# More unread products in the waits, norm sums behind additions, and columns ahead of the last turn in a four-layer model kernel

## The chip, the cores and the metric

The kernel runs on one core of a Trainium2 chip, in one launch. The metric is the device time of that launch in microseconds (us). The engines are PE (TensorE, matrix products), DVE (VectorE), ACT (ScalarE), POOL (GpSimd) and SP (SyncE, which issues transfers). Each runs its own queue in order, and semaphores join them.

## The reference

The input is 4 batches of 512 tokens, each token a row of 64 numbers. Four layers follow an embedding of atoms and their neighbours. Each has an attention and a feed-forward part, both on the residual stream `h`:

```
h = h + attn(layernorm(h))
h = h + ffn(layernorm(h))
```

- Layer 0: a causal linear attention with 8 heads, then 16 experts of which each token takes two, and a norm of its own.
- Layer 1: a softmax attention with one head over 512 keys, whose batches the kernel takes in pairs ("two-head" below), then a gate from a graph attention over 262144 edges and 4 experts of which two count.
- Layer 2: an attention over keys and values of 4 channels each with a 4x4 product per head, then 8 experts, two per token.
- Layer 3: 8 heads of softmax attention, then a block with a causal attention of 4 heads and 8 gated experts, two per token.

## The kernel before, in words

Tokens lie on the 128 partitions in 16 tiles of 128 tokens; a batch ("quarter" `q`, 0 to 3) is 4 tiles. `H` is the residual stream, `X` the normed one, and `XT2` is X turned, with channels on the partitions. PSUM has 8 banks of 128x512 numbers. The order of the work is written out by hand on every engine.

**Unread products.** At many places PE makes products of the identity with itself, 128x128 by 128x512 in bf16, that nobody reads (`dense` in `entry`, `unread` in the attentions). They keep PE active in a wait. They stand in PE's queue like any other product, so what follows must let them finish.

**`entry`** (line 2301) is what comes before a layer part: the norm in steps on DVE and ACT, the turn of X (L2534) and for experts the router or gate product (L2542). PE issues `dense` products first, then some after each step of quarter 0 (L2547). For experts, DVE then finds the two best experts and makes three bf16 terms of their weights (L2463, L2466), and PE turns the weights (L2584). Before that turn stands `turn_gates`: PE waits until DVE's steps for half 0 have come to `count - k` for k in 20, 14 and 8, and makes two unread products after each.

**`experts`** (line 1433) runs 4 x T tiles of experts in pairs: hidden layer (L1474), gates spread over the rows (L1485), ACT's function (L1543), DVE's product with the gate (L1571) and the second product (L1505). At the end of a quarter DVE sums two halves (L1577), PE turns them (L1512) and DVE adds them to the residual (L1562, L1564). If a norm follows (`after`), DVE makes its sums for quarter q (L2241, L2243) and later its root (L2260, L2262), and POOL centres, squares, takes the power and multiplies (L2251, L2254, L2269, L2272). So the first three quarters of the next norm are made within the experts, and the last quarter after them, with the last turn (`last_turn`).

**`softmax_attention`** (line 189) is the attention of layer 1: 2 groups `g` of 2 batches, 4 chunks `c` of 128 keys or queries each, step `s = 4g + c`. `rows` (L303) makes products whose maxima DVE takes (L488). After 4 chunks DVE splits the maxima in three bf16 terms (L497 to L505), PE turns them (`maxima`, L317), and ACT copies them (L432). `cols` (L329, L335) makes the products again, turned, with the maximum subtracted; ACT takes exponentials (L455), and `mix` (L351) multiplies by the values. `proj` (L291) makes queries and keys of a group from XT2, and needs both batches turned; the batches of group 1 are `first` (2) and `later` (3, the one whose norm ends last). `outs` (L362) is the head's output product. PSUM banks are given in the order of a list `units`, three pairs of banks in turn.

**`linear_attention`** (line 1158) handles 8 groups: products of keys and queries per chunk (`diagonals`, L1229), a turn of the keys (L1236), the running state (L1243), outputs within a chunk and across (L1254, L1263), and the head product (L1276).

**`l2_attn`** (line 3273): `kv(q)` (L3299) makes keys and values of a quarter, DVE adds a bias (L3459), ACT squares (L3405), DVE sums and scales (L3463 to L3472). `schedule` is the list of these steps.

## Time and profile before

| | |
|---|---|
| median of 3 runs | 909.41 us (908.62 to 911.94) |
| the profiled execution | 908.61 us, span 906.8 us |
| PE busy | 794.8 us, 88% of the span, 9110 products |
| DVE busy | 641.0 us, 71% |
| ACT busy | 367.0 us, 40% |
| POOL busy | 241.0 us, 27% |
| mean granted TensorE clock | 0.957 of 2.4 GHz |

The span runs from the first to the last instruction; what lies around it is 1.8 us. Busy shares are means over stages with different limits. Where PE is busy nearly without gaps and the granted clock is below full, its products themselves are slower. An unread product counts as busy.

### The profile page before, as it was taken

How to read it: one execution, taken by the hardware profiler on the slowest of the kernel's cores; microseconds unless marked ns; L12 is line 12 of the kernel's file. 1: busy time of each engine (PE TensorE's matmuls, PEld its weight loads, DVE VectorE, ACT ScalarE, POOL GpSimd, SP SyncE). 2: the span in 40 equal slices, each digit the busy share in tenths (PEclk: the TensorE clock that was granted, in tenths of full speed). 3: DMA queues.
4: the chain of work that ended last, by engine and by line, in shares of the span. 5: the costliest groups of instructions: out<-in, count | busy, mean ns of one | idle time of the engine just before them, and what ended most of it. 6: DMA issues, size and time to landing. Idle time of an engine off the chain costs nothing. (4 is left out here: it accounts for less than half of the span.)

```text
span 906.8 us, 21880 instructions
## 1 busy us (share of the span) xinstructions
PE 794.8 (88%) x9110; PEld 417.8 (46%) x9110; DVE 641.0 (71%) x1720; ACT 367.0 (40%) x633; POOL 241.0 (27%) x308
## 2 busy tenths in 40 slices
PE   0897879979999887997978989999999988888997
PEld 0566757755544335774445423333333333344443
DVE  3988648887897448998776885556565557666665
ACT  0213354444664243323444614555554432353443
POOL 1900003222645212441362041113133325110000
PEclk9898989998999999999899999999999999987999
DMA  9500030000000001000000000000000000000000
GB/s 280 170 1 2 1 98 3 3 3 2 1 2 2 1 2 50 1 2 1 1 1 2 1 2 1 1 3 2 1 2 1 2 1 3 3 2 1 7 7 13
DMA packets 11501, 15.40 MB, mean 17 GB/s; under 512 B 8390, under 2 KB 9446, under 8 KB 10406
## 3 DMA queue, kind: packets, MB, share of 16 engines
q1 hardware_dynamic: 9984, 12.91, 4.6%
q8 instruction: 72, 1.18, 0.5%
q10 hardware_dynamic: 1418, 1.09, 0.5%
q14 instruction: 27, 0.22, 0.1%
HBM read 13.47 MB, written 0.52 MB: 15 GB/s over the span
## 5 line engine op out<-in xcount | busy, mean ns | idle before, releaser
L1001 DVE TENSOR_REDUCE mx<-PS 128x2 f32<-128x1024 f32 (+3 forms) x96 | 103.1, 1088 | 65.8 <-PE PS L776 54.6
L947 ACT ACTIVATE arena<-PS 128x1024 f32<-128x1024 f32 (+3 forms) x96 | 85.8, 917 | 119.4 <-PE PS L820 107.7
L810 PE MATMUL PS<-arena 32*64 32x512 f32 (+3 forms) x768 | 86.3, 563 | 8.8 <-DVE mx L1001 2.9
L836 PE MATMUL PS<-arena 128*64 128x512 f32 (+3 forms) x384 | 91.1, 558 | 0.4 <-DVE arena L1060 0.4
L776 PE MATMUL PS<-arena 32*64 32x512 f32 (+3 forms) x768 | 85.6, 563 | 0.9 <-DVE mx L1001 0.4
L1543 ACT ACTIVATE arena<-PS,f_b_sb 128x512 f32<-128x512 f32 x96 | 61.1, 684 | 39.6 <-PE PS L1474 36.9
L1571 DVE TENSOR_TENSOR arena<-arena,PS 128x512 f32<-128x512 f32 x96 | 61.6, 683 | 15.6 <-PE PS L1485 15.5
L1474 PE MATMUL PS<-XT,late 64*64 64x512 f32 x384 | 63.0, 619 | 2.9 <-issue 1.5
L1505 PE MATMUL PS<-arena,late 64*64 64x512 f32 x384 | 57.9, 595 | 0.0
L1105 POOL TENSOR_TENSOR H<-H,arena 128x256 f32<-128x256 f32 x32 | 23.5, 733 | 114.3 <-DVE arena L1035 111.8
L1755 DVE TENSOR_TENSOR arena<-arena,PS 106x512 f32<-106x512 f32 (+1 forms) x48 | 30.8, 684 | 20.9 <-PE PS L1655 13.7
L810 PEld LDWEIGHTS PS<-arena 32*64 32x64 f32 x768 | 19.1, 130 | 55.9 <-issue 32.1
L2073 PE MATMUL PS<-late 128*128 128x128 fp8e5 x512 | 35.6, 234 | 8.4 <-DVE late L1982 8.4
L1723 ACT ACTIVATE arena<-PS 106x512 f32<-106x512 f32 (+1 forms) x48 | 26.0, 594 | 39.9 <-PE PS L1643 39.9
L2547 PE MATMUL PS<-identh 128*128 128x512 bf16 x80 | 27.4, 493 | 14.8 <-PEq L1198 4.0
L836 PEld LDWEIGHTS PS<-arena 128*64 128x64 f32 x384 | 19.7, 135 | 44.7 <-issue 38.5
L2073 PEld LDWEIGHTS PS<-late 128*128 128x128 fp8e5 x512 | 32.7, 106 | 13.2 <-DVE late L1982 11.1
L2269 POOL TENSOR_TENSOR st<-st,Cc 128x4 f32<-128x4 f32 x24 | 24.4, 1018 | 41.3 <-DVE st L2262 41.3
L3048 POOL TENSOR_TENSOR arena<-NB,vals 128x1280 f32<-128x1280 bf16 x11 | 25.7, 2339 | 34.9 <-DVE vals L3123 34.9
L1396 POOL TENSOR_TENSOR H<-H,arena 128x256 f32<-128x256 f32 x28 | 20.4, 728 | 53.4 <-DVE arena L1359 51.2
L1060 DVE SCALAR_TENSOR_TENSOR arena<-arena,Cc 128x256 f32<-128x256 f32 x32 | 15.5, 495 | 23.2 <-ACT arena L947 23.0
L1643 PE MATMUL PS<-XT,late 64*64 64x512 f32 (+1 forms) x192 | 30.4, 605 | 1.0 <-DVE L L2369 1.0
(482 smaller groups left out, 1718.4 us busy)
## 6 DMA issues: line engine op xcount, KB each, us to landing
arena<-in_rel SPq DMA_DIRECT2D x4, 1024.0 KB, 11.9
late<-in_edges SPq DMA_DIRECT2D x2, 1024.0 KB, 11.8
arena<-in_adj SPq DMA_DIRECT2D x1, 1024.0 KB, 6.8
late<-in_w_f_w SPq DMA_DIRECT2D x2, 512.0 KB, 3.9
Cc<-in_consts SPq DMA_DIRECT2D x1, 916.0 KB
arena<-in_ids ACTq DMA_DIRECT2D x1, 800.0 KB
late<-in_w_f_w SPq DMA_DIRECT2D x2, 340.0 KB, 3.7
late<-in_w_f_w SPq DMA_DIRECT2D x4, 128.0 KB, 2.9
```

The lines of the kernel that those rows point to most:

```text
L776: ins = nc.tensor.matmul(PS[half(m), a + j, keys(g, c)], QT[h, g % 3, of_chunk(c, m)], KT[h, g % 3, keys(g, c)], start=True, stop=not late ...
L810: ins = nc.tensor.matmul(PS[half(m), a + j, queries(g, c)], KT[h, g % 3, of_chunk(c, m)], QT[h, g % 3, queries(g, c)], start=not less_firs ...
L836: ins = nc.tensor.matmul(PS[half(j), 6 + p, queries(g, c)], XO[:, batch(g) * TB + c, :], PT[:, s % 2, p, j, queries(g, c)], start=c == 0, ...
L947: nc.scalar.activation(PT[:, s % 2, p, :, queries(g, c)], PS[:, a:a + 2, queries(g, c)], ACT.Exp, scale=of(g).scale).then_inc(exp_done.sem, 1)
L1001: v.reduce_max(mx[:, g % 2, c, 2 * p:2 * p + 2], PS[:, a:a + 2, keys(g, c)], axis=AX.X).then_inc(max_done.sem, 1)
L1474: ins = nc.tensor.matmul(PS[half(m), up_bank(n), :], w1(i)[r, half(m)], XT2[r, b * S:(b + 1) * S], start=True, stop=True, skip_group_check ...
L1505: ins = nc.tensor.matmul(PS[half(i), banks[m], :], w2(i)[half(m)], HG[half(m), n % 4, :], start=m == 1 and i < 2, stop=i >= T - 2, skip_gr ...
L1543: nc.scalar.activation(HA[:, n % 3, :], PS[:, up_bank(n), :], act_fn, bias=b1(tiles[n][1])).then_inc(hidden_done.sem, 1)
L1571: v.tensor_tensor(HG[:, n % 4, :], HA[:, n % 3, :], PS[:, gate_bank(n), :], ALU.mult).then_inc(gated_done.sem, 1)
L1643: ins = nc.tensor.matmul(PS[m, z, :], w1(*tile)[half(z), m], XT2[half(z), b * S:(b + 1) * S], start=True, stop=True, skip_group_check=True)
L1755: nc.vector.tensor_tensor(HG[0:rows_of(r), n % 4, :], HA[0:rows_of(r), n % 3, :], PS[0:rows_of(r), 2 + z, :], ALU.mult).then_inc(gated_don ...
L2073: ins = nc.tensor.matmul(PS[:, 6 + m % 2, n * P:(n + 1) * P], spelt[k % 3][:, g, P:2 * P], spelt[k % 3][:, g, 0:P], start=g % GROUP == 0, ...
```

## The change

- `entry`: 8 unread products at the head instead of 4, unless there are two norms with a sum (5 there, as before). This touches five of the entries.
- `turn_gates`: unread pairs after seven marks, k = 20, 14, 12, 10, 8, 6, 4, instead of three; 14 products instead of 6, in all four expert layers.
- `linear_attention`: 14 unread products instead of 8 ahead of the first group, and 4 more between its diagonals and its turn.
- `experts` with 4 tiles per quarter (layers 1 and 2): the norm's sums stand right behind the addition of their quarter, and no longer behind the gating and the summing of that turn of the loop.
- `softmax_attention`: the order is written for two groups. The maxima are turned, and two steps of columns made, before `later` is turned and group 1 projected. 3 unread products stand in the first wait instead of 6. ACT takes the exponentials of steps 0 and 1 ahead of the copies for group 1. POOL copies values of batches 0 and 1 between its steps of the last norm.
- `l2_attn`: quarter 2 is turned behind `kv(1)` and the queries, ACT copies it behind the first square, and the root of the last norm stands one step earlier in DVE's queue.

```diff
@@ softmax_attention, the order of PSUM banks
+        first, later = new_in(1)
+        units = [("N", q, 0) for q in new_in(0)] + [("P", 0, 0)] + [("A", s, 0) for s in range(TB)]
+        units += [("N", first, 0), ("T", 0, 0), ("B", 0, 0), ("B", 1, 0), ("N", later, 0), ("P", 1, 0)]
+        units += [("B", 2, 0), ("A", TB, 0), ("A", TB + 1, 0), ("B", 3, 0), ("A", TB + 2, 0), ("A", TB + 3, 0), ("T", 1, 0)]
+        units += [("B", TB, 0), ("B", TB + 1, 0), ("O", 0, 0), ("B", TB + 2, 0), ("B", TB + 3, 0), ("O", 1, 0)]
@@ softmax_attention, PE
                 for s in range(TB):
                     rows(s)
-                first, later = new_in(1)
                 entered.turn(eng, first, slot(("N", first, 0)))
-                unread(6, a=7)
-                entered.turn(eng, later, slot(("N", later, 0)))
+                unread(3, a=7)
                 maxima(0)
-                proj(1)
                 eng.wait_ge(out_added.sem, before["out_added"])
                 eng.wait_ge(xo_ready.sem, at(xo_ready, 1))
...
+                cols(0)
+                cols(1)
+                mix(0, 0)
+                entered.turn(eng, later, slot(("N", later, 0)))
+                proj(1)
+                cols(2)
+                mix(1, 0)
+                rows(TB)
+                rows(TB + 1)
+                cols(3)
+                mix(2, 0)
+                rows(TB + 2)
+                rows(TB + 3)
+                mix(3, 0)
+                maxima(1)
+                for s in range(TB, U):
+                    cols(s)
+                    if s > TB:
                         mix(s - 1, 0)
...
+                    if s == TB + 1:
+                        outs(0, 0)
+                mix(U - 1, 0)
@@ softmax_attention, ACT
+                    if s == 1:
+                        entered.turned_out(eng, later, bank(("N", later, 0)))
+                        qk(1)
+                    if s == 3:
+                        contexts(0)
+                        maxima(1)
@@ softmax_attention, POOL
-                if len(entered.norms) > 1:
-                    entered.centre(eng, B - 1, 1)
-                    entered.apply(eng, B - 1, 1)
-                for b in range(B):
+                values_out(0)
+                entered.centre(eng, B - 1, 1)
+                values_out(1)
+                entered.apply(eng, B - 1, 1)
+                for b in range(2, B):
                     values_out(b)
@@ linear_attention, PE
-                unread(8, 6)
+                unread(14, 6)
...
                     diagonals(g)
+                    if g == 0:
+                        unread(4, 6)
                     turn(g)
@@ experts, DVE
+        short = T == 2 * LAG
...
                         v.tensor_tensor(dst[:, y, :], turned[:, :, 1], dst[:, y, :], ALU.add).then_inc(out_added.sem, 1)
+                        if after is not None and short and b < B - 1:
+                            eng.wait_ge(out_added.sem, a0 + b + 1)
+                            after.sums(eng, b, 0)
...
-                            if e == 0:
+                            if e == 0 and not short:
@@ entry, PE
-                    dense(5 if len(norms) > 1 and norms[0].plus is not None else 4)
+                    dense(5 if len(norms) > 1 and norms[0].plus is not None else 8)
...
-                    for k in (20, 14, 8):
+                    for k in (20, 14, 12, 10, 8, 6, 4):
                         eng.wait_ge(gate_steps[0].sem, gate_steps[0].count - k)
                         dense(2)
@@ l2_attn, PE
                 kv(0)
-                entered.turn(eng, 2, turn_bank(2))
                 kv(1)
                 queries(0)
                 queries(1)
+                entered.turn(eng, 2, turn_bank(2))
                 kv(2)
@@ l2_attn, ACT
-                for q in range(B - 1):
+                for q in range(2):
                     entered.turned_out(eng, q, turn_bank(q))
...
+                        if q == 0:
+                            entered.turned_out(eng, 2, turn_bank(2))
@@ l2_attn, DVE
-                    if (k, q) == (2, 0):
+                    if (k, q) == (1, 0):
                         entered.root(eng, B - 1, 0)
```

The order of PE's queue in the two-head attention, from the first turn for group 1 to the rows of its first two steps. Names are those of the code: `Cc,X` is a turn of X, `identh` alone an unread product, `XT,late` the projection. Before:

```order
L2294 MATMUL PS<-Cc,X 64x128 x8
L368 MATMUL PS<-identh 128x512 x6
L2294 MATMUL PS<-Cc,X 64x128 x8
L317 MATMUL PS<-identh,arena 128x128 x4
L291 MATMUL PS<-XT,late 64x512 x4
L329 MATMUL PS<-arena 64x512 x4
L335 MATMUL PS<-arena,minus 64x512 x4
L303 MATMUL PS<-arena 64x512 x8
```

In the changed kernel, whose own line numbers stand here (L2263, L348, L297, L271, L309, L315, L331 and L283 are the lines above, with L331 the `mix`):

```order
L2263 MATMUL PS<-Cc,X 64x128 x8
L348 MATMUL PS<-identh 128x512 x3
L297 MATMUL PS<-identh,arena 128x128 x4
L309 MATMUL PS<-arena 64x512 x4
L315 MATMUL PS<-arena,minus 64x512 x4
L309 MATMUL PS<-arena 64x512 x4
L315 MATMUL PS<-arena,minus 64x512 x4
L331 MATMUL PS<-arena 64x512 x4
L2263 MATMUL PS<-Cc,X 64x128 x8
L271 MATMUL PS<-XT,late 64x512 x4
```

The second turn and the projection moved from ahead of the first columns to behind two steps of them and one `mix`.

The order of ACT's queue in the key-value attention, from its first copy. `XT<-PS` is the copy of a turned quarter, `arena<-arena` the square. Before:

```order
L2299 COPY XT<-PS 128x512 x3
L3405 ACTIVATE arena<-arena 128x512
L3414 ACT_TABLE_LOAD
L3414 ACTIVATE chan<-chan 128x128
L3405 ACTIVATE arena<-arena 128x512
```

In the changed kernel:

```order
L2268 COPY XT<-PS 128x512 x2
L3374 ACTIVATE arena<-arena 128x512
L2268 COPY XT<-PS 128x512
L3385 ACT_TABLE_LOAD
L3385 ACTIVATE chan<-chan 128x128
L3374 ACTIVATE arena<-arena 128x512
```

The third quarter's copy moved behind the first square, still ahead of the table load.

PE's queue at the gates of the second expert layer, between the first hidden products and the first spread of gates. Before:

```order
L1474 MATMUL PS<-XT,late 64x512 x6
L2547 MATMUL PS<-identh 128x512 x6
L2584 MATMUL PS<-identh,G 64x128 x32
L1485 MATMUL PS<-GT,pickh 64x512 x4
L1474 MATMUL PS<-XT,late 64x512 x2
```

In the changed kernel:

```order
L1440 MATMUL PS<-XT,late 64x512 x6
L2516 MATMUL PS<-identh 128x512 x14
L2553 MATMUL PS<-identh,G 64x128 x32
L1451 MATMUL PS<-GT,pickh 64x512 x4
L1440 MATMUL PS<-XT,late 64x512 x2
```

Eight unread products more stand ahead of the turn of the gates; nothing else moved.

## Rows read from the trace of the kernel before

**Rows 1.** Stretches: window, length, busy (count) PE PEld DVE ACT POOL, PEclk, DMA share, GB/s

```profile
125.00:131.80 6.80, 5.58 (x23) 3.56 (x25) 4.60 (x10) 1.66 (x4) 0.00 (x0) 0.50 0.11 24
...
210.30:217.10 6.80, 6.80 (x49) 2.65 (x40) 5.80 (x40) 2.85 (x6) 0.00 (x0) 0.50 0.01 2
...
302.50:305.90 3.40, 3.22 (x18) 1.33 (x18) 0.00 (x0) 1.12 (x2) 0.95 (x5) 0.50 0.00 0
...
428.80:435.60 6.80, 6.13 (x58) 3.21 (x62) 4.69 (x14) 3.33 (x7) 1.21 (x5) 0.50 0.01 2
...
811.00:817.80 6.80, 6.00 (x39) 3.84 (x39) 5.88 (x20) 4.12 (x11) 0.00 (x0) 0.50 0.01 2
...
824.70:834.90 10.20, 7.82 (x58) 3.57 (x55) 6.78 (x39) 3.92 (x7) 0.00 (x0) 0.50 0.01 2
```

**Rows 2.** Timeline: start, length, engine, line, operation, count [idle before]; norm before linear attention

```profile
109.92 2.33 PE L2547 MATMUL PS<-identh 128*128 128x512 bf16 x10
...
111.89 0.40 DVE L2353 TENSOR_TENSOR X<-tA,st 128x256 f32<-128x256 f32 x1
...
112.34 3.71 PE L2534 MATMUL PS<-Cc,X 128*64 128x128 f32 x64
```

**Rows 3.** Timeline, linear attention, its first group, PE

```profile
119.52 1.90 PE L1268 MATMUL PS<-identh 128*128 128x512 bf16 x8
...
123.39 1.17 PE L1229 MATMUL PS<-arena 32*128 32x128 f32 x32 [1.97 <-DVE arena L1342]
...
125.66 0.90 PE L1236 MATMUL PS<-Cc,arena 128*128 128x128 f32 x3 [1.09 <-DVE arena L1342]
...
127.12 1.76 PE L1243 MATMUL PS<-arena 128*128 128x192 f32 x6 [0.57 <-ACT arena L1320]
```

**Rows 4.** Timeline, PE in the gates of the first expert layer

```profile
212.68 2.74 PE L2547 MATMUL PS<-identh 128*128 128x512 bf16 x6
...
215.35 1.91 PE L2584 MATMUL PS<-identh,G 128*64 128x128 bf16 x32
```

**Rows 5.** Timeline, two-head attention, PE and one row of DVE

```profile
296.76 1.47 PE L368 MATMUL PS<-identh 128*128 128x512 bf16 x6
...
301.71 1.30 PE L2294 MATMUL PS<-Cc,X 128*64 128x128 f32 x16 [3.48 <-POOL X L2272]
...
302.19 0.27 DVE L505 CAST arena<-mrest 128x8 bf16<-128x8 f32 x1
...
315.22 1.04 PE L329 MATMUL PS<-arena 64*64 64x512 f32 x8
...
317.91 0.38 PE L317 MATMUL PS<-identh,arena 128*128 128x128 bf16 x4 [0.58 <-DVE arena L505]
...
318.97 1.09 PE L329 MATMUL PS<-arena 64*64 64x512 f32 x8 [0.68 <-ACT arena L432]
```

**Rows 6.** Timeline, PE in the gates of the second expert layer

```profile
429.47 1.92 PE L2584 MATMUL PS<-identh,G 128*64 128x128 bf16 x32 [1.11 <-DVE G L2463]
...
435.59 0.59 PE L1505 MATMUL PS<-arena,late 64*64 64x512 f32 x2
```

**Rows 7.** Timeline, PE in the gates of the third expert layer

```profile
501.85 2.44 PE L2547 MATMUL PS<-identh 128*128 128x512 bf16 x6
...
504.22 1.08 PE L2584 MATMUL PS<-identh,G 128*64 128x128 bf16 x32
...
508.27 0.59 PE L1505 MATMUL PS<-arena,late 64*64 64x512 f32 x2
```

**Rows 8.** Timeline, ACT and PE in the key-value attention

```profile
460.83 0.58 ACT L2299 COPY XT<-PS 128x512 f32<-128x512 f32 x1 [3.37 <-PE PS L2294]
...
466.20 1.09 PE L2294 MATMUL PS<-Cc,X 128*64 128x128 f32 x16 [1.28 <-POOL X L2272]
```

**Rows 9.** Timeline, PE in the norm and the gates of the last expert layer

```profile
814.12 3.68 PE L2534 MATMUL PS<-Cc,R 128*64 128x128 f32 x32 [0.23 <-DVE R L2355]
...
828.55 1.92 PE L2584 MATMUL PS<-identh,G 128*64 128x128 bf16 x32 [0.95 <-DVE G L2463]
```

79 lines of the change are left out of this document (6 added, 73 removed).

## The prediction

> **What bounds the kernel now.** I read the page's busy shares first: PE is busy for 88% of the span, so the end is set by PE nearly everywhere, and what counts is where PE waits and how fast its clock is. The slices of the granted clock show short dips, and the view of stretches places them [rows 1]. In each of these six the granted clock is 0.50, which is 1.2 GHz, and PE is busy for 35.6 of their 40.8 us. I then read the timeline around each, to see what PE did just before the clock fell. Each time it had waited: for DVE in the linear attention [rows 3], 3.48 us for POOL's last norm in the two-head attention [rows 5], for DVE's gate steps in the experts [rows 6, 9]. So the change is worth what it takes from waits and from half-clock work, less what its own products hold up.
>
> **Prices.** Eight unread products take 1.90 us and six 1.47 at full clock [rows 3, 5], so one more costs (1.90 - 1.47) / 2 = 0.215 us. At half clock six take 2.74 [rows 4], some 0.43 us each without the tail.
>
> **1. Norm ahead of the linear attention, +4 products.** Ten unread products end at 112.25, X is ready at 112.29, and the turn starts at 112.34 [rows 2]. The last product's tail overlaps its follower by some 0.2 us, so about 0.26 us is spare. 4 x 0.215 = 0.86, less 0.26: **+0.6 us**. Ends: 0 if PE has more slack, +0.9. In the other four entries the products stand before a turn that ACT's copies, behind a table load, or DVE's steps hold up anyway: 0; were that cover gone, +0.6 each.
>
> **2. Linear attention, +6 and +4 products.** They stand in waits of 1.97 and 1.09 us [rows 3]; 6 x 0.215 = 1.29 and 4 x 0.215 = 0.86 fit, so nothing is held up. Behind them comes the half-clock stretch from 125.0, with PE busy 5.58 of 6.8 us [rows 1]. At full clock half of that goes, 2.8 us at most; L1243 alone would fall from 1.76 us to 0.9 [rows 3]. Part of it lies beside ACT and DVE. **-2.0**, ends 0 and -2.8.
>
> **3. Gates of the first expert layer, +8 products.** Here the clock is at half from 210.3 to 217.1 [rows 1], because of a wait ahead of L1474 that the change leaves alone. The six products start at 212.68 and the turn follows at once, at 215.35 [rows 4]: no room is left. Fourteen make ten by 217.1, and four at full clock end at about 217.9. The turn then takes 1.08 instead of 1.91 us [rows 4, 7] and ends at 219.0, not at 217.26: **+1.7**. All eight at half clock would cost 3.4; with full clock from the start they fit into DVE's steps, 0.
>
> **4. Two-head attention, new order.** PE now waits 3.48 us for the turn of `later`, and the split of the maxima ends at 302.46 [rows 5]. In the new order `maxima(0)` is next, and it cannot start before 302.5 whatever the order, since DVE's split stands behind POOL's norm as before. With 3 unread products instead of 6 PE runs dry at about 297.6 and waits 4.9 us. The maxima come 0.4 us earlier, but at 302.5 the turn, most of it done before, is still to be made (-0.4, +0.8). New waits: the first columns wait for ACT's copy of the maxima, 0.7, like the 0.68 in front of the later columns [rows 5], where the projection used to fill in; the projection waits for ACT's copy of the turn, 0.58 for a copy [rows 8], 0.5 taken. At `maxima(1)`, columns and `mix` of step 3 stood between the last rows and the turn, 2.1 us from 315.22, and 0.58 were left [rows 5]. Now only `mix(3)`, some 0.9, stands there, and two rows in a row make DVE's maxima later by 0.4: a wait of 2.0. Against this, `mix(4)` no longer waits (-0.4). Sum: -0.4 + 0.8 + 0.7 + 0.5 + 1.4 - 0.4 = 2.6, and I take **+2.5**. Ends: -0.4, if the queues behind PE take up all the waits, and +4.2, with another half-clock stretch behind the second wait (half of 3.22 us of PE work [rows 1]).
>
> **5. Gates of the second expert layer.** Of the eight new products two go before 425.3 and six after 427.3, in waits. The turn starts at 429.47 after an idle 1.11 us for DVE's G [rows 6], so they hold nothing up. From its start to L1505 it is 6.12 us at half clock [rows 6], and 4.05 in the third layer at full clock [rows 7]. **-2.0**, ends 0 and -2.1.
>
> **6. Layer 1 experts into key-value attention.** The sums behind the addition put the norms of quarters 1 to 3 about 1.3 us ahead, while L1571 and L1577 come 0.6 later, where PE has other work. ACT no longer waits 3.37 us for the turn of quarter 2 before its first square [rows 8]. The last turn, at 466.20 after 1.28 us for POOL [rows 8], comes some 2.7 earlier, but DVE's chain is the bound from there: **-1.4**, ends 0 and -3. What is late next is `kv(3)`. In layer 2 the same move gains about 1 us for the norms, but its one early turn and the last turn wait for the sum that now comes later: 0, ends -0.5 and +0.8.
>
> **7. Gates of the third expert layer.** As in 3: six products from 501.85, the turn at 504.22 without a wait [rows 7]. Eight more, four of them at half clock or so: **+1.6**, ends 0 and +3.4.
>
> **8. Norm of the last expert layer, +4.** They stand in a wait, and the turn that follows takes 3.68 us at a granted clock of 0.50 [rows 1, 9], about 1.9 at full. **-1.6**, ends 0 and -2.0.
>
> **9. Gates of the last expert layer.** The products run until about 829.1, past 828.55 (+0.55), where the turn now starts after 0.95 us idle [rows 9]. But PE is busy 7.82 of 10.2 us at half clock here [rows 1], and some 4.5 of that would be at full clock: **-1.7**, ends +1.6 and -3.0.
>
> Sum: 0.6 - 2.0 + 1.7 + 2.5 - 2.0 - 1.4 + 0 + 1.6 - 1.6 - 1.7 = -2.3 us. The profiled execution took 908.61 us, so 906.3; the median of the runs is 0.8 above it, so the forecast is **907.1 us**.
>
> **A rule on the clock.** In this trace the half clock comes behind waits, though not behind every one: the 3.48 us wait brought it, the waits around 317 did not [rows 1, 5]. The Trainium skill (TensorE: Matmul & The Clock Gate, Part 1: The HAM clock gate) says that the activity is measured in a free-running period that does not start with the kernel, so that the same kernel turns slow or fast at other points from run to run. One trace cannot show it. By it terms 3 and 7 could be 0 in one run and 3.4 in the next; this speaks against more products where the clock may be low, and is the first rival.
>
> **The rivals.** (a) *The slow stretches lie elsewhere.* If the clock is full at 212 and 501, the fourteen products fit into DVE's steps, terms 3 and 7 are 0, and PE gains another half microsecond in each. With -2.8 in term 2, +1.5 in term 4, -2.1 in 5 and -2.4 in 9 the sum is 0.6 - 2.8 - 0.5 + 1.5 - 2.1 - 1.4 - 0.5 - 1.6 - 2.4 = -9.2: 900.2 us. For it: three of these are already the mild end of their rows. Against it: the waits ahead of terms 3 and 7 are untouched. (b) *The two-head attention loses more: slower.* The longer wait of 4.9 us and the new one of 2.0 ahead of `maxima(1)` each end in a half-clock stretch, and term 4 is +4.2. It decides from the point where the second wait passes about 2 us, against 0.58 now [rows 5]; if then the products of 2, 5, 8 and 9 bring only a half of their gain, the sum is 0.6 - 1.0 + 1.7 + 4.2 - 1.0 - 1.4 + 1.6 - 0.8 - 0.4 = +3.5, and with term 3 and 7 at their ends (+3.4) +7.0: 916.4 us. (c) *The change does not lift the clock.* The stretches stay where they are, terms 2, 5, 8 are 0 and 9 is +1.0: 0.6 + 1.7 + 2.5 - 1.4 + 1.6 + 1.0 = +6.0, 915.4 us. Against it: in term 2 the unread products nearly fill the waits ahead of the stretch.
>
> **How the numbers follow.** The forecast has a chance of 0.54, (a) 0.28, (b) 0.10, (c) 0.08. A measurement of this kernel can tell about 0.5%, 4.5 us, from no change: faster is below 904.9, slower above 913.9. All of (a) and little of the forecast's own lower flank are faster, 0.30; (c) and (b) lie about that upper bound, and half of their milder forms fall below it: slower 0.11; the rest, 0.59, within. The range reaches from 901.5, near (a), to 912.5, short of (b) and (c).
>
> **What the changed profile would show.** Right: granted clock 1.0 in the first group of the linear attention, behind the gates of the second and last expert layers and in the last norm's turn; two-head columns that start at about 303.8 on this trace's scale, but a wait of some 2 us before the second turn of maxima; the kv attention's last turn without a wait for POOL. The unread products of the first and third gates end after DVE's G is ready. Wrong: a two-head attention that is no longer than before, which would mean that PE was not its bound; or a mean clock still at 0.957.

## The result, and the profile after

The changed kernel is slower: a median of 913.83 us over 20 executions against 909.46 for the kernel before, ratio 1.0047 (95% interval 1.0027 to 1.0067), so +4.3 us where -2.3 was forecast. The executions of the changed kernel lie between 907.4 and 918.5 us, those of the kernel before between 903.5 and 918.1 us. Ratios here and below compare fast executions only, that is, those within 1.5% of the fastest of the same kernel. The profiled one took 917.40 us, span 915.6. Its page, the busy shares and the slices of the granted clock:

```profile
span 915.6 us, 21998 instructions
...
PE 812.5 (89%) x9169; PEld 426.2 (47%) x9169; DVE 641.4 (70%) x1720; ACT 367.2 (40%) x633; POOL 243.3 (27%) x308
...
PEclk9886999989999798999998898999999999998999
```

PE is busy for 17.7 us more than before. To see where, I cut both traces at the same products: without the unread ones both kernels issue the same 8920, in another order only inside the two stages that were rewritten. A stretch is what lies between two such cuts. Here is the view of stretches before, its columns as in [rows 1]. The rows are, in this order, the norm ahead of the linear attention, the latter's first groups, norm and gates of layer 0, the two-head attention, the graph attention's first part, the gates of layer 1, its experts and the key-value attention, the gates of layer 2, its last experts, the attention of layer 3, and norm and gates of its experts:

```profile
99.49:112.83 13.34, 10.73 (x136) 8.08 (x137) 9.46 (x42) 5.99 (x18) 1.99 (x1) 1.00 0.01 1
112.83:137.68 24.85, 19.72 (x252) 14.05 (x252) 12.34 (x23) 13.30 (x25) 1.16 (x2) 0.86 0.30 89
...
190.30:232.38 42.08, 34.85 (x387) 20.84 (x381) 32.29 (x139) 20.59 (x39) 13.68 (x10) 0.88 0.01 2
...
282.88:331.02 48.14, 41.49 (x398) 17.29 (x394) 20.63 (x42) 16.50 (x23) 15.42 (x27) 0.96 0.00 1
331.02:373.15 42.13, 34.20 (x369) 24.59 (x369) 36.98 (x115) 14.76 (x34) 12.69 (x13) 0.96 0.09 28
...
408.00:443.82 35.82, 31.28 (x216) 16.09 (x217) 28.22 (x138) 14.83 (x26) 8.10 (x20) 0.90 0.00 1
443.82:495.62 51.80, 42.25 (x404) 24.86 (x398) 38.05 (x87) 22.93 (x47) 23.47 (x26) 0.93 0.01 1
495.62:525.81 30.19, 28.18 (x270) 13.66 (x270) 24.64 (x113) 15.58 (x26) 3.94 (x6) 0.94 0.00 1
525.81:543.99 18.18, 15.97 (x120) 4.91 (x116) 15.03 (x26) 3.32 (x6) 6.97 (x15) 1.00 0.01 1
543.99:805.33 261.34, 247.76 (x3360) 89.73 (x3364) 156.95 (x290) 117.44 (x153) 68.86 (x94) 0.99 0.01 2
805.33:843.87 38.54, 31.90 (x280) 17.45 (x273) 26.90 (x130) 15.18 (x31) 0.00 (x0) 0.78 0.01 1
```

The same stretches after:

```profile
104.01:118.04 14.03, 11.50 (x140) 8.47 (x141) 10.12 (x45) 6.67 (x19) 1.99 (x1) 1.00 0.00 1
118.04:140.36 22.32, 19.45 (x263) 13.38 (x262) 11.66 (x20) 12.69 (x24) 1.16 (x2) 1.00 0.32 100
...
192.94:235.42 42.48, 36.29 (x399) 21.39 (x393) 32.26 (x139) 20.60 (x39) 13.68 (x10) 0.88 0.01 2
...
285.89:338.82 52.93, 42.47 (x395) 18.27 (x391) 20.41 (x42) 16.65 (x23) 15.43 (x27) 0.90 0.00 1
338.82:382.05 43.23, 36.15 (x372) 25.83 (x373) 36.95 (x115) 14.76 (x34) 12.69 (x13) 0.92 0.08 27
...
416.88:450.71 33.83, 30.75 (x223) 15.62 (x224) 28.17 (x138) 14.62 (x26) 8.07 (x20) 1.00 0.01 1
450.71:501.28 50.57, 43.50 (x408) 25.26 (x402) 39.57 (x87) 23.16 (x47) 23.46 (x26) 0.90 0.00 1
501.28:535.18 33.90, 31.17 (x279) 14.54 (x278) 26.53 (x118) 15.58 (x26) 5.17 (x8) 0.90 0.01 1
535.18:552.65 17.47, 16.01 (x118) 4.89 (x115) 13.80 (x22) 3.32 (x6) 5.75 (x13) 1.00 0.01 1
552.65:816.20 263.55, 251.17 (x3361) 90.49 (x3365) 156.97 (x290) 117.45 (x153) 68.62 (x94) 0.97 0.01 2
816.20:852.80 36.60, 31.26 (x293) 16.12 (x284) 26.85 (x130) 15.09 (x31) 0.00 (x0) 0.91 0.01 2
```

The bounds show one thing at once: the first stretch begins 4.5 us later after (104.01 against 99.49), and nothing of the change stands ahead of it. Those 4.5 us belong to this one execution. From there on the difference is +4.4 us, which is what the medians say. Stretch by stretch, the two-head attention has +4.8, the gates of layer 2 +3.7, the attention of layer 3 +2.2 with unchanged code, the graph attention +1.1 with only the four further unread products of its entry, and the norm and the gates of layer 0 +0.7 and +0.4. Against them stand -2.5, -2.0, -1.9, -1.2 and -0.7. The four that grew by more than 1 us have a lower granted clock than before, and the two-head attention has waits too. This is the timeline of PE in it, columns as in [rows 2], to be read against [rows 5]:

```profile
299.78 0.82 PE L348 MATMUL PS<-identh 128*128 128x512 bf16 x3
305.62 0.58 PE L297 MATMUL PS<-identh,arena 128*128 128x128 bf16 x4 [5.02 <-DVE arena L467]
307.08 1.99 PE L309 MATMUL PS<-arena 64*64 64x512 f32 x8 [0.88 <-ACT arena L404]
...
314.96 1.47 PE L271 MATMUL PS<-XT,late 64*64 64x512 f32 x5 [0.73 <-ACT XT L2268]
...
326.96 0.38 PE L297 MATMUL PS<-identh,arena 128*128 128x128 bf16 x4 [1.91 <-DVE arena L467]
328.02 1.09 PE L309 MATMUL PS<-arena 64*64 64x512 f32 x8 [0.68 <-ACT arena L404]
```

The four waits that term 4 named are there with the sizes it gave: 5.0 us (4.9), 0.88 and 0.73 for ACT (0.7 and 0.5), 1.91 (2.0). What it had not counted is the clock: the same eight column products take 1.99 us at 307.08 and 1.09 at 328.02. The granted clock is at half from 302.7 to 313.0, so all of PE's work from the maxima to the first `mix` runs at half clock.

### The profile page after: what moved, and what is told of

Same layout as the page of the kernel before. It is cut to its first block and busy times, and to the rows that moved or that the text cites. A ratio compares the mean times of both kernels' runs of the same rounds, so it can differ in the third digit from the quotient of the medians.

```text
span 915.6 us, 21998 instructions
## 1 busy us (share of the span) xinstructions
PE 812.5 (89%) x9169; PEld 426.2 (47%) x9169; DVE 641.4 (70%) x1720; ACT 367.2 (40%) x633; POOL 243.3 (27%) x308
## 3 DMA queue, kind: packets, MB, share of 16 engines
q10 hardware_dynamic: 1418, 1.09, 0.5%
## 5 line engine op out<-in xcount | busy, mean ns | idle before, releaser
L799 PE MATMUL PS<-arena 128*64 128x512 f32 (+3 forms) x384 | 93.4, 571 | 0.4 <-DVE arena L1023 0.4
L2516 PE MATMUL PS<-identh 128*128 128x512 bf16 x132 | 40.7, 467 | 12.0 <-PEq L1161 4.0
L2042 PE MATMUL PS<-late 128*128 128x128 fp8e5 x512 | 37.9, 243 | 7.1 <-DVE late L1951 7.1
L2042 PEld LDWEIGHTS PS<-late 128*128 128x128 fp8e5 x512 | 34.9, 110 | 12.0 <-DVE late L1951 8.2
L2516 PEld LDWEIGHTS PS<-identh 128*128 128x128 bf16 x132 | 14.1, 115 | 40.1 <-issue 22.4
```

The lines of the kernel that those rows point to most:

```text
L799: ins = nc.tensor.matmul(PS[half(j), 6 + p, queries(g, c)], XO[:, batch(g) * TB + c, :], PT[:, s % 2, p, j, queries(g, c)], start=c == 0, ...
L2042: ins = nc.tensor.matmul(PS[:, 6 + m % 2, n * P:(n + 1) * P], spelt[k % 3][:, g, P:2 * P], spelt[k % 3][:, g, 0:P], start=g % GROUP == 0, ...
L2516: nc.tensor.matmul(PS[:, 6, :], identh[:], bc(identh[:], 1, TB), start=True, stop=True, skip_group_check=True)
```

## The experiments

There were sixteen runs of thirteen further kernels, in four sets of four on two chips, each set beside the kernel before on the same chip. For each I give the stretches above in its own trace. "Half clock" is time at a granted clock of 0.50. A section at the end takes all executions together, by their mean time at half clock, which is 2 x (1 - granted clock) x span.

### Chance and the change

**changed_again**: no edit.

> The changed kernel once more, nothing edited, for a second trace of it. In the first pair of traces 5.0 of the 8.9 us between the kernels lie ahead of the first line that the change touches: 20.5 us of half clock between 63.8 and 84.3 us, against 6.8 us in the kernel before. Theory A (where the half clock lies is partly chance, and the change did not bring this): the second trace has about 6.8 to 10 us of half clock ahead of 100 us, reaches the norm of the linear attention within 1 us of the kernel before, and its span lies near 911. Theory B (the changed program sets it): again about 20 us of half clock there. Both expect the two-head attention to cost some 4.8 us more than before and a ratio to the kernel before of about 1.0047.

Ratio 1.0021 (0.9975 to 1.0066). Theory A holds in what it says of the clock: 10.2 us of half clock ahead of the first bound, not 27.3 as in the first trace after. The bound came at 97.89 us, 1.6 ahead of the kernel before, and the span was 907.1 us, not 911. From the first bound to the end it is +2.0 us. The two-head attention took 53.41 us, +5.3. In the eighteen traces of this study the first bound lay between 97.9 and 105.8 us, though the code ahead of it is the same in all. The four latest, 103.2 us and more, belong to traces with 23.9 to 27.3 us of half clock ahead of it; the others, with 10.2 to 23.9, lie between 97.9 and 102.2 and do not follow it closely.

### The two-head attention

**two_head_back**: the functions of the two-head attention as before.

```diff
-                unread(3, a=7)
+                unread(6, a=7)
+                entered.turn(eng, later, slot(("N", later, 0)))
                 maxima(0)
+                proj(1)
...
```

> The changed kernel with the two-head attention in its old order (PE, ACT, POOL, list of banks, 6 unread products), all other parts as changed. In the traces the new order took 4.8 us more between the first turn of its group 1 and the first output product, with 10.2 us of half clock instead of 3.4. Theory A: the new order is the whole loss, so the stage takes again what it took before, the kernel gains 4 to 5 us on the changed one, and is within 1 us of the kernel before, or below it by up to 1 (ratio about 0.999). Theory B: the other parts lose as well, and the ratio stays above 1.001. Theory C (my forecast): the order costs 2.5, the other parts gain 4.8, ratio 0.995.

**two_head_filled**: `unread(3, a=7)` becomes `unread(20, a=7)` in the changed kernel.

> The changed kernel with 20 unread products instead of 3 in the wait of 5.0 us ahead of the first turn of maxima. 20 x 0.215 = 4.3 us, so at full clock they end inside the wait. Theory A (the loss is mainly the half clock that the empty wait brings): the granted clock is 1.0 from the maxima to the projection, 7.3 us of PE work at half clock become about 4, and the stage is 3 to 3.5 us shorter than in the changed kernel; what is left of the 4.8 is the 1.9 us wait ahead of the second turn of maxima. Theory B (the order itself costs, because columns wait for ACT and the maxima of group 1 come later): the stage gets shorter by under 1 us, whatever the clock.

**order_only**: the kernel before with only the hunks of `softmax_attention`.

> The kernel before with the new two-head order alone (PE, ACT, POOL, list of banks, 3 unread products), all else as before. The stretch from the late experts' first products of this stage to the last steps (two segments, 48.1 us in before, 53.0 to 53.4 in three changed kernels) should be 52.9 to 53.4 again. Theory A (the order's cost is what the stage shows): the kernel is slower than before by 4.8 to 5.3 us, ratio 1.005 to 1.006. Theory B (the order also brings half clock in later stages, as the difference of 8.5 us between the mean spans of changed_again and two_head_back says): ratio 1.008 to 1.010.

**old_order_filled**: two_head_back with 18 for 6 unread products.

> The changed kernel with the old two-head order and 18 unread products instead of 6 in its wait of 3.5 us for POOL's last norm: 12 x 0.215 = 2.6 us, which fit. Theory A (the empty wait brings the half clock behind it): the granted clock is 1.0 from the second turn to the columns, and the stretch from the first products of group 1 to the last steps gets 1.0 to 1.6 us shorter than in two_head_back (48.45 us from its rows to its end); ratio about 0.992. Theory B: the clock falls there anyway, and nothing changes.

**new_order_two_fills**: two_head_filled with three marks in layers 0 and 2, and in `maxima(1)`, behind its wait for the bank:

```diff
+                    if g == 1:
+                        unread(8, a)
```

> The changed kernel with marks as in marks_in_two_layers, the new two-head order, 20 unread products in its first wait and 8 ahead of the second turn of maxima, where PE waited 1.9 us at full clock: 8 x 0.215 = 1.7. In two_head_filled the stage took 50.1 us. Theory A (there the clock was full already, so the second fill buys nothing): 50.0 to 50.3 us, and the kernel is 1.0 to 1.7 us slower than marks_in_two_layers. Theory B (the second wait had cost clock further on): less half clock behind the stage, and the kernel comes level with marks_in_two_layers, ratio 0.987.

| kernel | ratio | two-head attention, us | at half clock there |
|---|---|---|---|
| before | 1 | 48.1 | 3.4 |
| linear_only (below) | 0.9993 | 49.5 | 6.8 |
| order_only | 1.0050 (1.0028 to 1.0073) | 52.6 | 6.8 |
| changed (two traces) | 1.0047, 1.0021 | 52.9, 53.4 | 10.2, 10.2 |
| two_head_back | 0.9931 (0.9897 to 0.9965) | 48.5 | 3.4 |
| two_head_filled | 0.9972 (0.9941 to 1.0002) | 50.1 | 0 |
| new_order_two_fills | 0.9980 (0.9950 to 1.0009) | 51.5 | 3.4 |
| old_order_filled | 0.9924 (0.9892 to 0.9957) | 46.9 | 0 |

The stretch in two_head_filled and in old_order_filled, and, between the two, PE's longest waits in the former:

```profile
283.70:333.81 50.11, 43.28 (x413) 19.09 (x408) 20.40 (x42) 16.67 (x23) 15.44 (x27) 1.00 0.00 1
```

```profile
303.43 0.38 PE L297 MATMUL PS<-identh,arena 128*128 128x128 bf16 x4 [1.35 <-DVE arena L467]
304.69 1.09 PE L309 MATMUL PS<-arena 64*64 64x512 f32 x8 [0.88 <-ACT arena L404]
...
321.95 0.38 PE L297 MATMUL PS<-identh,arena 128*128 128x128 bf16 x4 [1.90 <-DVE arena L467]
```

```profile
283.54:330.44 46.90, 42.63 (x411) 18.07 (x407) 20.63 (x42) 16.44 (x23) 15.42 (x27) 1.00 0.01 1
```

With 20 unread products the clock is full, and the stage is 2.8 us shorter than in the first trace after and 3.3 shorter than in changed_again, though PE does 17 products more. That is near theory A's 3 to 3.5, and 2.0 us against before are left. But the stage before has 3.4 us of half clock of its own. At full clock on both sides the new order costs 50.1 - 46.9 = 3.2 us, and the traces with 6.8 us at half clock on both sides agree: 52.6 in order_only against 49.5 in linear_only, +3.1. That is the price of its waits. The rest of the +4.8, 1.6 us, is the clock (2.1 of the +5.3).

The old order has no fixed share of half clock either: 3.4 us in before, sums_only, no_marks_in_two_layers and both runs of two_head_back (48.1 to 48.5 us), 6.8 in linear_only, seven_marks_in_three and both runs of marks_in_two_layers (49.3 to 49.5). The new order with 3 unread products has 10.2 in all four traces with the rest of the change (52.9 to 53.4) and 6.8 in order_only. Nor does all of it come behind the first wait. In the first trace after it does. In changed_again, gates_three_marks and changed_two_layers 6.8 us lie at the first wait and 3.4 begin some 2 us behind the second turn of maxima. In changed_again:

```profile
321.68 1.95 PE L309 MATMUL PS<-arena 64*64 64x512 f32 x8
```

order_only and two_head_filled had the same second wait of 1.9 us and no half clock behind it.

In the kernels' times the order turns a gain into a loss. With the old one back the changed kernel runs at 0.9931, and at 0.9950 in the second run of it below; my other terms alone had given 0.995 (theory C). order_only is slower by 4.5 us in the stage and by its ratio (4.6 us), which is theory A's account, though the stage took 52.6 us and not 52.9 or more; theory B's further loss in later stages is not in its ratio. old_order_filled is 1.6 us shorter in the stage than two_head_back, theory A, but no faster as a kernel beyond the intervals; one of its twelve executions took 2593 us and is left out. In new_order_two_fills the 8 products filled the second wait to its end and the stage got no shorter: 51.5 us, with 3.4 us at half clock ahead of that fill, where two_head_filled had none. Its 50.0 to 50.3 (theory A) was missed, and the trace has that stretch for it. Theory A's time of the kernel was missed too, and so was theory B's 0.987: 13.7 us of half clock came in the stage behind. This run does not say what the second wait costs by itself.

### The gates

**gates_three_marks**: `for k in (20, 14, 8):` in all four layers of the changed kernel.

> The changed kernel with unread pairs after three marks of DVE's gate steps again, not seven: 6 products instead of 14 in each of the four expert layers. Theory A (the forecast): the eight products hold up the turn of the gates where PE is at half clock behind them (first and third expert layer, +1.7 and +1.6) and save half-clock work in the second and last (-2.0 and -1.7), so the kernel stays within 1 us of the changed one. In the traces these four were +0.4, -2.0, +3.0 and -1.9. Theory B: the products gain everywhere the clock is full at their start and the kernel gets slower by 2 us or more without them. Theory C: they lose on balance, and it gets faster by 1 to 3 us.

**marks_in_two_layers** and, once more, **two_layers_again**: two_head_back with the marks taken per expert layer:

```diff
+MARKS = cycle([(20, 14, 8), (20, 14, 12, 10, 8, 6, 4), (20, 14, 8), (20, 14, 12, 10, 8, 6, 4)])
...
-                    for k in (20, 14, 12, 10, 8, 6, 4):
+                    for k in next(MARKS):
```

> The changed kernel with the old two-head order, and with the seven marks in the second and last expert layer only; the first and third have three marks, 6 products, as before. Against the kernel two_head_back this takes 16 products out of the two layers where PE has no wait to fill. Theory A: the layers gain 0.5 us each where the clock is full and 3 us where it is half; ratio 0.989 to 0.992, below the 0.9931 of two_head_back. Theory B (fewer products there let the clock fall right behind): no faster than two_head_back, ratio 0.993 to 0.996.

> marks_in_two_layers once more: its 0.9866 came from 6 executions. Theory A (sixteen products less in the first and third expert layer save 3 us or more): ratio 0.985 to 0.989 again, half clock of 50 to 58 us in nearly all executions. Theory B (those six were a lucky phase of the clock): 12 executions spread as in the other kernels, ratio 0.990 to 0.993, level with two_head_back_again.

**two_head_back_again**, on the chip of two_layers_again:

> two_head_back once more on the same chip as two_layers_again, for the comparison of the two. Theory A: 0.992 to 0.994, slower than two_layers_again by 3 to 6 us. Theory B: the two within 2 us.

**seven_marks_in_three**: marks_in_two_layers with seven marks in the third layer too. **changed_two_layers**: the changed kernel with the marks of marks_in_two_layers. **no_marks_in_two_layers**: marks_in_two_layers with empty lists for the first and third layer.

> The old two-head order, seven marks in the second, third and last expert layer, three in the first: it parts term 3 of the forecast (first layer) from term 7 (third). In the traces the third layer's entry and gates took 33.9 us with fourteen products and 6.8 us of half clock, 32.2 with six and as much half clock; the first layer's 42.5 and 41.6 likewise. Theory A (both hold up their turn, the third more): 1 to 2 us slower than two_layers_again, faster than two_head_back_again by 1 us. Theory B (chance alone): level with both within 1.5 us.

> The changed kernel, new two-head order and all, with three marks in the first and third expert layer and seven in the others. changed_again had 1.0021, gates_three_marks (three marks everywhere) 0.9985. Theory A (the first and third layer's sixteen products lose, the other sixteen gain): below both, 0.994 to 0.997. Theory B (they make no difference beyond chance): 0.998 to 1.003.

> marks_in_two_layers without any unread product at the gates of the first and third expert layer. Theory A (six products there buy no clock and hold the turn up where they run at half clock): the two gate stretches take 0 to 1 us less, 41.0 to 41.6 and 30.0 to 31.5 us. Theory B (without them a longer half-clock stretch follows): each takes 1 to 2 us more.

| kernel | ratio | products in layers 0 and 2 | norm and gates of layer 0, us (half clock) | of layer 2 |
|---|---|---|---|---|
| changed | 1.0047 | 14, 14 | 42.5 (10.2) | 33.9 (6.8) |
| changed_again | 1.0021 | 14, 14 | 42.0 (6.8) | 33.9 (6.8) |
| gates_three_marks | 0.9985 (0.9947 to 1.0023) | 6, 6 | 41.5 (10.2) | 30.7 (0) |
| changed_two_layers | 0.9947 (0.9913 to 0.9981) | 6, 6 | 41.5 (10.2) | 30.7 (0) |
| two_head_back | 0.9931 | 14, 14 | 42.7 (10.2) | 34.0 (6.8) |
| two_head_back_again | 0.9950 (0.9919 to 0.9982) | 14, 14 | 42.6 (10.2) | 33.9 (6.8) |
| seven_marks_in_three | 0.9944 (0.9920 to 0.9968) | 6, 14 | 41.5 (10.2) | 33.9 (6.8) |
| marks_in_two_layers | 0.9866 (0.9834 to 0.9898) | 6, 6 | 41.6 (10.2) | 32.2 (6.8) |
| two_layers_again | 0.9908 (0.9872 to 0.9943) | 6, 6 | 41.7 (10.2) | 32.2 (6.8) |
| no_marks_in_two_layers | 0.9998 (0.9974 to 1.0022) | 0, 0 | 43.6 (17.1) | 34.0 (13.7) |
| two_head_filled | 0.9972 | 14, 14 | 42.6 (10.2) | 31.0 (0) |

Among kernels with the other changes, traces with as many products and as much half clock agree within 0.25 us. Fourteen products against six cost 1.0 us in layer 0 and 1.5 to 1.7 in layer 2 at the same time at half clock, and 0.3 in layer 2 where the clock was full. PE in layer 2 of the changed kernel, and of two_head_filled:

```profile
508.56 4.35 PE L2516 MATMUL PS<-identh 128*128 128x512 bf16 x14
512.84 1.08 PE L2553 MATMUL PS<-identh,G 128*64 128x128 bf16 x32
```

```profile
501.33 3.20 PE L2516 MATMUL PS<-identh 128*128 128x512 bf16 x14
504.46 1.08 PE L2553 MATMUL PS<-identh,G 128*64 128x128 bf16 x32
```

Yet none at all is no better than fourteen: worse by 1.0 us in layer 0, level in layer 2, and each 1.8 to 2.0 us longer than with six, theory B of that run. In no_marks_in_two_layers PE waits 3.40 us for the gates of layer 0 and does everything behind them at half clock, to 226 us:

```profile
214.42 2.23 PE L1479 MATMUL PS<-XT,late 64*64 64x512 f32 x12 [1.34 <-issue]
220.05 1.92 PE L2592 MATMUL PS<-identh,G 128*64 128x128 bf16 x32 [3.40 <-DVE G L2471]
...
222.33 1.91 PE L1479 MATMUL PS<-XT,late 64*64 64x512 f32 x4
```

So six there are better than fourteen and better than none, by the stages. The kernels' times are less clear. With the old order, seven marks in two layers gave 0.9866 against 0.9931 for seven in all four, each against its own runs of before; the second time, on one chip, 0.9908 against 0.9950, with intervals that overlap. Seven marks in two layers rest on 6 and 7 executions. That speaks for theory A of marks_in_two_layers. But 0.9908, with a mean of 62 us at half clock, is theory B's number for two_layers_again: the first 0.9866 was in part luck. seven_marks_in_three, at 0.9944, lies where two_head_back_again does, which neither of its theories says.

gates_three_marks, at 0.9985, is on the side of theory C, not clear of noise. It took 35.9 us for the gates of layer 1 (half clock 6.8), every kernel with seven marks there 33.8 (none). Against linear_only and sums_only, which have six products there and only 3.4 us at half clock, 33.8 is 0.7 to 0.9 less, so the eight further products earn 0.7 to 2.0 us in layer 1. In layer 3 no trace shows that they earn anything: norm and gates took 36.6 us with six products in gates_three_marks and 36.6 with fourteen in the first trace after, both with 6.8 us at half clock. changed_two_layers, at 0.9947, is theory A, and clear of noise: with the new two-head order kept, the changed kernel is faster than the one before once layers 0 and 2 have six products.

### The rest, one part at a time

**linear_only**: the kernel before with the two hunks of `linear_attention`. **sums_only**: with the three hunks of `experts`.

> The kernel before with the 6 and 4 further unread products of the linear attention alone; everything else is as before, so the trace is also a second look at the rest of the kernel before. In four traces of kernels with the whole change the stretch from the turn of the norm ahead of the linear attention to the start of its later groups took 22.3 us, against 24.9 before. Theory A (these ten products end the half clock there): 22.3 to 22.5 us here too, and 1.5 to 2.5 us less in all. Theory B (the four further products at the entry are what keeps the clock up): near 24.9 us. For the rest: if the half clock at the gates of layers 0 and 2, in the first 100 us and around 550 us lies elsewhere than in the first trace of before, chance sets it; if it comes at the same places, the program does.

> The kernel before with the norm's sums right behind the addition, for the experts of layers 1 and 2, and nothing else. In the traces the stretch from the late experts of layer 1 to the first products of the key-value attention took 13.2 us in all four kernels with the whole change, 16.1 before. Theory A (the earlier sums bring it): 13.2 to 13.7 us here. Theory B (the order of ACT and of the turn in the key-value attention brings it): near 16.1 us. My forecast had given both together 1.4 us.

linear_only: ratio 0.9993 (0.9961 to 1.0026), the linear attention's first groups 22.32 us at a granted clock of 1.00, which is theory A; what it gains is below what the ratio resolves. In the rest of it, whose code is that of before, the half clock lay elsewhere: 23.9 us ahead of the first bound for 13.7, 13.7 at the gates of layer 0 for 10.2, 6.8 in the two-head attention for 3.4. sums_only: ratio 0.9957 (0.9934 to 0.9980). The stretch of the layer 1 experts and the key-value attention took 51.4 us in linear_only, 50.0 in sums_only, and 49.3 in changed_again: -1.4 for the sums, though 3.4 us of that trace were at half clock. With 3.4 us there too, changed_two_layers took 49.3, so the order of ACT and the turns brings -0.7. The expectation's own, shorter segment took 14.8, between its 16.1 and 13.2; its end is a product that the order moves, so it can't part the two. The last experts of layer 2 took 17.5 instead of 18.2 us wherever the sums stood early.

**two_layers_and_filled**: marks_in_two_layers with 18 unread products for 6 in the old two-head order.

> marks_in_two_layers with 18 unread products instead of 6 in the wait of the old two-head order: the two edits that helped, together. In old_order_filled the stage took 46.9 us (28.06 of it behind the rows), in marks_in_two_layers 49.3. Theory A (they add up): 46.9 us in the stage, a kernel 1.5 to 2.5 us faster than marks_in_two_layers, ratio 0.984 to 0.986. Theory B (half clock only moves to another place, as the 10.2 us behind that stage in old_order_filled suggest): the stage is shorter and the graph attention behind it longer by 2 us, ratio 0.986 to 0.989.

Ratio 0.9926 (0.9900 to 0.9952). The traces are as theory B has it, but the ratio is worse than its number: 46.9 us in the stage, and the graph attention behind it 44.1 instead of 42.2, the attention of layer 3 264.9 instead of 261.3.

### All executions together

| kernel | executions | mean at half clock, us | mean span | span at 70 us of half clock |
|---|---|---|---|---|
| before (both chips) | 128 | 88 | 909.8 | 904.5 |
| order_only | 12 | 94 | 915.4 | 908.2 |
| changed | 20 | 81 | 912.3 | 908.9 |
| changed_again | 12 | 77 | 911.2 | 909.1 |
| two_head_filled | 12 | 60 | 905.8 | 908.9 |
| new_order_two_fills | 12 | 69 | 908.2 | 908.6 |
| gates_three_marks | 12 | 80 | 908.7 | 905.6 |
| changed_two_layers | 12 | 65 | 905.1 | 906.7 |
| two_head_back | 12 | 57 | 903.2 | 907.2 |
| two_head_back_again | 12 | 62 | 904.1 | 906.4 |
| old_order_filled | 11 | 64 | 904.9 | 906.6 |
| seven_marks_in_three | 12 | 64 | 903.9 | 905.7 |
| marks_in_two_layers | 6 | 51 | 899.8 | 905.3 |
| two_layers_again | 7 | 62 | 901.8 | 904.1 |
| two_layers_and_filled | 12 | 69 | 904.3 | 904.6 |
| no_marks_in_two_layers | 12 | 88 | 911.0 | 905.5 |
| linear_only | 12 | 92 | 911.0 | 904.4 |
| sums_only | 12 | 86 | 907.9 | 903.2 |

Within one kernel a microsecond more at half clock goes with 0.30 us more of span (one slope through the executions of all eighteen sets); the last column moves each mean along it. It is an estimate, good to about 0.5 us for twelve executions, and it parts what the work costs from what the clock costs. All the change but the order adds 2 to 3 us of work and waits, and takes away some 28 us of half clock, worth 8. The new order adds another 2 and gives back 20 us of half clock, worth 6; put into the kernel before (order_only) it adds 3.7 us and only 6 us of half clock. two_head_filled shows that the empty first wait is what brings the half clock: with that wait filled the kernel has the same span at equal clock as the changed one, but 60 us at half instead of 80.

## Why the prediction was wrong

**The step that failed is term 4**, the two-head attention: +2.5 forecast, +4.5 with the order alone, +4.8 and +5.3 in the changed kernel. Each wait was there with the size that I gave it, yet at equal time at half clock they cost 3.1 to 3.2 us together, 0.5 to 0.6 more than the sum of 2.6. The larger part of the miss is the clock, which the sum left out. I put it into the upper end only ("with another half-clock stretch behind the second wait"). I had made the first wait longer myself, from 3.5 to 4.9 us with half the unread products in it, and took no charge for that, although rows 1 and 5 show a half-clock stretch already behind 3.5 us. In the trace after, the work behind it went at half clock for 7.3 us instead of 3.4; in three further traces there was less of it behind the first wait, and a stretch behind the second. In the changed kernel the price does not end with the stage: the order brought about 20 us of half clock per execution (estimate), of which the stage holds 7.

**Rival (b)** had the mechanism, the place and nearly the price (+4.2), with a chance of 0.10. Its sum of +3.5 would be 912.9 us; 913.83 was measured. That is partly luck, since it had the gains of terms 2 and 5 halved, and they came whole. Whether its decider, the second wait, matters is not shown: 1.9 us long, it had half clock behind it in three of the six traces that left it empty, and none in the other three. With the first wait filled the stage had no half clock in one trace and 3.4 us in another; filling the second as well bought nothing more.

The other terms, in us, forecast and measured in the first pair of traces:

| term | forecast | measured | what the runs show besides |
|---|---|---|---|
| 1 norm, +4 | +0.6 | +0.7 | the same in every trace with it |
| 2 linear attention | -2.0 | -2.5 | alone: -2.5 |
| 3 gates, layer 0 | +1.7 | +0.4 | +1.0 for the eight products at equal clock, -0.5 for the entry's four |
| 5 gates, layer 1 | -2.0 | -2.0 | 33.8 us in every trace with them; before 35.8, or 34.5 to 34.8 with less half clock |
| 6 sums, key-value attention | -1.4 | -1.2, -0.7 | -1.4 the sums, -0.7 the order, and -0.7 in layer 2 |
| 7 gates, layer 2 | +1.6 | +3.7 | +1.5 to +1.7 at equal clock, +0.3 at full |
| 8, 9 last norm and gates | -3.3 | -1.9 | -3.3 where the clock was at half for 3.4 us, -1.9 where for 6.8 |
| attention of layer 3, and graph attention | 0 | +3.3 | the clock: 0 for the graph attention's four more products at equal clock |

**Terms 1, 2, 5** and the price of a product (0.215) held to 0.5 us. **Term 3** was too dear: the stretch at half clock there was 3.4 us long, not 6.8, and the fourteen products took 4.5 us, not 5.2. **Term 7** was right as to its eight products. Of the other 2 us, 1.5 are the trace that it was set against: 30.2 us there, but 31.7 in linear_only and order_only, whose code in that stage is that of before; the rest is open. **Term 6** was right for the sums; what I gave layer 2, nothing, was -0.7. **Terms 8 and 9** have two values in the traces with seven marks, 35.1 to 35.3 and 36.5 to 36.6 us against 38.5 before; the forecast's -3.3 is the first. But order_only, without any of these products, had 35.0, and gates_three_marks, without the eight of the gates, 36.6: how much of that gain is theirs is open, and for term 9's products no trace shows any.

**Rival (a)** asked for full clock at the gates of layers 0 and 2. Layer 0 had it in changed_again and old_order_filled. There the fourteen products took 3.2 us and PE still waited for the gates behind them, and the stage took 42.0 and 41.9 us, against 42.1 before. In changed_again:

```profile
208.77 3.20 PE L2516 MATMUL PS<-identh 128*128 128x512 bf16 x14
212.53 1.10 PE L2553 MATMUL PS<-identh,G 128*64 128x128 bf16 x32 [0.57 <-DVE G L2432]
```

So they cost nothing there, as this rival says. Layer 2 had full clock in two_head_filled, where they cost +0.3, not 0. Neither kernel came near its 900.2 us as a median. **Rival (c)** fell: the stretches of terms 2 and 5 went in every trace with their products.

**What the forecast left out**: stretches at half clock in code that nothing had touched. In the attention of layer 3 two of them came, 24 us apart, in both traces of the changed kernel, in gates_three_marks, seven_marks_in_three, two_head_back_again and old_order_filled, and not in before, linear_only, sums_only and order_only. In changed_again:

```profile
748.20:751.60 3.40, 3.40 (x40) 1.56 (x36) 3.19 (x11) 0.66 (x2) 1.00 (x2) 0.50 0.00 0
772.10:775.50 3.40, 3.40 (x45) 1.34 (x34) 3.07 (x10) 0.66 (x2) 0.00 (x0) 0.50 0.00 0
```

PE is busy in them without a gap, but not ahead of them. In the 3.4 us before the clock fell, PE had idled for 1.3:

```profile
744.80:748.20 3.40, 2.06 (x42) 0.94 (x38) 2.95 (x4) 0.00 (x0) 1.60 (x2) 1.00 0.00 0
```

The code of this stage is the same everywhere, and its time lay between 259.6 and 264.9 us with 0 to 17.1 us at half clock. two_head_back has none of it in its first trace and all 13.7 us in its second, so the kernel's text alone does not set it. The six traces with these two stretches, and only they, also have an earlier one that begins 5.8 to 6.1 us behind the first product of the stage; where another has one it begins at 4.7 to 5.6 or 7.6 to 7.8 us. So the three stretches come as one pattern, and the pattern as a whole comes or stays away. The Trainium skill (TensorE: Matmul & The Clock Gate, Part 1: The HAM clock gate) says that the gate watches PE in a free-running period that the start of a kernel does not reset. That one kernel has the pattern in one execution and not in another agrees with it; whether the change makes the pattern likelier is open, and no run sets it alone.

**The range** (901.5 to 912.5) was too narrow by its upper side: it took one trace's clock for the kernel's, while the executions of before lie 14.6 us apart. The prediction had named a mean clock of 0.957 as a sign of being wrong; it was 0.949. Its signs of being right came too, from the full clock in the linear attention to the key-value attention's last turn without a wait for POOL; none of them looked at the clock behind the first wait.

## What to carry to other kernels

Price a wait of PE twice: by its length, and by the work behind it that will run at half clock. In this kernel each microsecond at half clock went with 0.30 us of time. Whoever moves work out of a long wait to close another should fill what is left with unread products; but not past the time at which the waited-for data come, least of all where the clock is already at half, for there a product costs 0.43 us and lies on the path. And one trace of such a kernel tells its work, not its clock, nor what stands behind which wait: cut several traces at the same instructions, and compare stages at equal time at half clock. A stage compared with one trace of before looked 1.5 us worse than it was, and the last layer's gate products looked like a gain that no trace shows to be theirs.

## What was unexpected in the hardware

A busy PE alone did not hold the clock, nor bring it back. In the first trace after, PE was busy for all of the 3.4 us before the clock fell, and for all of the next 13.6 us at half clock; the work was products of 128x128 fp8 and of 64x64 fp32. The half clock lasted 20.5 us. In the trace before, the same 20.5 us had a mean of 0.83.

```profile
60.40:63.80 3.40, 3.40 (x37) 3.30 (x35) 1.04 (x1) 0.00 (x0) 0.00 (x0) 1.00 0.00 0
63.80:77.40 13.60, 13.60 (x87) 13.17 (x87) 4.09 (x15) 2.31 (x5) 0.00 (x0) 0.50 0.00 1
63.80:84.30 20.50, 19.26 (x136) 18.29 (x135) 10.92 (x42) 2.31 (x5) 0.00 (x0) 0.50 0.00 1
```

The Trainium skill, in the same section, ties the clock to how busy PE has been; by the profile's busy time, these rows do not agree. And more filling is not more clock: old_order_filled had no half clock in the two-head attention and 10.2 us of it in the stage behind, 3.4 in before. sums_only, with nothing filled, had 10.2 there too, so the fill need not be what brought it.
